# Layer 2 of a graph stack: pairs of tiles times two weights at once, in seven block products

## The reference

```python
def _L2_gnn_ref(X, A, Wv, bv, aw, ab, Wk, bk):
    Xw = X @ Wv + bv
    sj = Xw @ aw[:d, 0]
    si = Xw @ aw[d:, 0]
    e = leaky_relu(sj[:, None, :] + si[:, :, None] + ab[0], negative_slope=0.2)
    alpha_matrix = A * exp(e)
    transition = alpha_matrix / (sum(alpha_matrix, axis=-1, keepdims=True) + 1e-12)
    H = 0; Xk = X
    for k in range(3):
        H = H + Xk @ Wk[k] + bk[k]
        Xk = einsum('bij,bjd->bid', transition, Xk)
    return relu(H)
```

## Time and profile before

| | us |
|---|---|
| median of 3 runs | 2690.77 (2690.70 to 2690.77) |
| the profiled execution | 2691.02 |
| its span, first to last instruction | 2689.2 |
| TensorE busy | 2649.0 (99%) |
| VectorE busy | 1896.2 (71%) |
| ScalarE busy | 1217.6 (45%) |
| GpSimd busy | 1153.2 (43%) |

### The profile page before, as it was taken

How to read it: one execution, slowest core, us unless ns; L and a number is a source line. 1 busy time by engine, 2 the same in 40 slices (tenths; PEclk the granted TensorE clock), 3 DMA queues, 4 the chain that set the end, 5 groups by cost and what they waited for, 6 DMA issues and landing times.

```text
span 2689.2 us, 44559 instructions
## 1 busy us (share of the span) xinstructions
PE 2649.0 (99%) x13154; PEld 2210.4 (82%) x13154; DVE 1896.2 (71%) x4376; ACT 1217.6 (45%) x2231; POOL 1153.2 (43%) x2022
## 2 busy tenths in 40 slices
PE   7999999999999999999999999999999999999999
PEld 4888888888888888888888887888888888888887
DVE  7777777777777665666666657777777777777776
ACT  4444444444444554545445454323223222666665
POOL 5444443444444634343333346212212122677776
PEclk9999999999999999999999999999999999999999
DMA  4111111111111312111211123111111112344443
GB/s 135 41 37 47 41 37 37 42 46 37 38 36 45 98 46 67 33 66 36 64 41 59 45 73 102 58 55 54 51 57 49 55 55 64 114 148 152 137 138 123
DMA packets 136299, 178.58 MB, mean 66 GB/s; under 512 B 54464, under 2 KB 54464, under 8 KB 136256
## 3 DMA queue, kind: packets, MB, share of 16 engines
q1 hardware_dynamic: 131072, 168.62, 19.5%
q10 hardware_dynamic: 5184, 9.44, 1.2%
HBM read 110.90 MB, written 67.11 MB: 66 GB/s over the span
## 4 chain that ended last, share of the span: by engine, by line
PE 94%; DVE 2%; ACT 1%; issue 1%; POOL 1%; DMA 0%; SPq 0%; POOLq 0%; ACTq 0%; DVEq 0%
PE ps L461 27%; PE ps L463 27%; PE ps L462 27%; PE ps L478 6%; PE ps L503 4%; PE ps L481 2%; POOL w_lo L1261 1%; ACT row_hi L695 0%; DVE row_lo L945 0%; ACT w_hi L695 0%; PE ps L581 0%; PE ps L577 0%; DMA raw<-w0a 0%; POOL vecs L1286 0%; DVE adj_both L945 0%
## 5 line engine op out<-in xcount | busy, mean ns | idle before, releaser
L461 PE MATMUL ps<-w_hi,col_hi 128*128 128x512 f32 x2752 | 1100.8, 400 | 3.5 <-POOL w_lo L1261 1.0
L463 PE MATMUL ps<-w_hi,col_lo 128*128 128x512 f32 x2752 | 1075.4, 391 | 0.0
L462 PE MATMUL ps<-w_lo,col_hi 128*128 128x512 f32 x2752 | 1072.5, 390 | 0.0
L463 PEld LDWEIGHTS ps<-w_hi,col_lo 128*128 128x128 f32 x2752 | 516.8, 188 | 112.9
L461 PEld LDWEIGHTS ps<-w_hi,col_hi 128*128 128x128 f32 x2752 | 517.1, 188 | 109.9 <-issue 5.1
L462 PEld LDWEIGHTS ps<-w_lo,col_hi 128*128 128x128 f32 x2752 | 518.3, 188 | 98.5 <-issue 0.2
L1294 POOL TENSOR_TENSOR var_eps<-moments,eps_ln 128x1 f32<-128x1 f32 x256 | 55.6, 217 | 918.8 <-DVE moments L962 918.8
L695 ACT ACTIVATE col_hi<-ps 128x512 fp32r<-128x512 f32 x448 | 255.8, 578 | 257.2 <-PE ps L481 134.0
L949 DVE TENSOR_TENSOR wide<-ps,col_hi 128x512 f32<-128x512 f32 x256 | 175.5, 686 | 146.8 <-ACT col_hi L695 145.3
L695 ACT ACTIVATE row_hi<-ps 128x512 fp32r<-128x512 f32 x224 | 133.3, 595 | 305.7 <-PE ps L463 304.3
L1261 POOL TENSOR_TENSOR row_lo<-normed,row_hi 128x512 fp32r<-128x512 f32 x128 | 165.2, 1301 | 214.1 <-ACT row_hi L695 214.1
(11 more groups left out here) (151 smaller groups left out, 4095.1 us busy)
## 6 DMA issues: line engine op xcount, KB each, us to landing
out<-x_res SPq DMA_DIRECT2D x256, 256.0 KB, 2.0
x_in<-out SPq DMA_DIRECT2D x192, 256.0 KB, 2.8
x_in<-x SPq DMA_DIRECT2D x64, 256.0 KB, 2.6
x_res<-out SPq DMA_DIRECT2D x64, 256.0 KB, 3.1
adj_in<-adj_t SPq DMA_DIRECT2D x96, 64.0 KB, 2.4
raw<-w ACTq DMA_DIRECT2D x12, 256.0 KB, 2.7
raw<-wk ACTq DMA_DIRECT2D x12, 256.0 KB, 2.7
raw<-w_t ACTq DMA_DIRECT2D x10, 256.0 KB, 3.0
```

Of the source, the lines that this page charges most:

```text
L461: nc.tensor.matmul(out_ap, lhs_hi, rhs_hi, start=start, stop=False, **checks)
L462: nc.tensor.matmul(out_ap, lhs_hi, rhs_lo, start=False, stop=False, **checks)
L463: return nc.tensor.matmul(out_ap, lhs_lo, rhs_hi, start=False, stop=stop, **checks)
```

## The change

In layer 2, Wk2 and Wk1 are put side by side and a pair of tiles is multiplied by both in the seven block products of layer 3 (`halved` on each engine now serves both layers; `seventh` takes the layer). `lin2` and `lin1` go; `lin0` stays a linear per tile.

- The lists of layers 1 to 3 are new, and the last groups' lists of all four are written out. In layer 2's the products of one pair of tiles stand between the mixes and `lin0` of the other.
- `sj`, `alpha` and `tt` work on pairs: two transposes in a row, one step of ACT over both tiles.
- The score with vi: POOL multiplies (step `score`), ACT sums; DVE keeps the one with vj.
- `seed`: ACT copies the bias `bk` into the bank of `lin0` before it starts. `adj0`: ACT takes the relu, POOL adds the residual, which is now loaded by SP (`load_residual`) instead of copied.
- `adj1`: DVE adds the mix to the corner, ACT and POOL split the sum.
- The normalisation writes in place (`x_in`), and the loads of the next group's x wait for the transposes and scores.
- Weights: 32 operands in `STEPS`, made at places of the lists given in `STAGING` (layer, group, place): twelve in layer 1's groups 0 and 1, six in its last group, two in layer 2's first, and the twelve of `FINAL` (layer 3's) in layer 2's last group, each into the place of a layer 2 operand once the last pair's product has used it (`TAKES`). DVE makes the differences (`make`), ACT the high part, POOL the low part (`stage`).
- Group 1 also runs outside the loop, which now covers groups 2 to 14.

```diff
 def order_diffuse():
     return [
...
+        ("stats_n", 0), ("seed", 1), ("p1", 1), ("p2", 1), ("stats_n", 1), ("adj1", 0), ("adj1", 1), ("p6", 1),
+        ("seed", 0), ("norm_n", 0), ("p5", 1), ("lin0", 1), ("norm_n", 1), ("seed", 3), ("c11", 1), ("s5", 1),
+        ("sj", 1), ("alpha", 1), ("lin0", 0), ("score_n", 0), ("score_n", 1), ("tr_n", 0), ("p7", 1), ("c11h", 1),
+        ("c22", 1), ("sums_n", 0), ("tt", 1), ("tr_n", 1), ("adj0", 0), ("adj0", 1), ("p3", 1), ("sumsplit_n", 0),
+        ("p4", 1), ("stats_n", 2), ("c21", 1), ("p1_n", 0), ("stats_n", 3), ("seed", 2), ("p2_n", 0), ("c11_n", 0),
+        ("norm_n", 2), ("adj1", 2), ("p6_n", 0), ("adj1", 3), ("s5_n", 0), ("norm_n", 3), ("sj_n", 0), ("alpha_n", 0),
+        ("lin0", 3), ("score_n", 2), ("score_n", 3), ("c22_n", 0), ("p5_n", 0), ("lin0", 2), ("tr_n", 2),
+        ("sums_n", 1), ("adj0", 2), ("tr_n", 3), ("p7_n", 0), ("tt_n", 0), ("adj0", 3), ("p3_n", 0), ("c11h_n", 0),
+        ("sumsplit_n", 1), ("c21_n", 0), ("p4_n", 0),
     ]
...
 # module
+QUARTERS = ("B11", "B12", "B21", "B22")
+EARLY = [(2, op, j) for j in range(2) for op in ("B21", "B11", "T1", "T2", "T3", "T4")]
+LATE = [(2, "W0", j) for j in range(4)] + [(2, "B22", j) for j in range(2)] + [(3, "B11", j) for j in range(2)]
+FINAL = [(3, op, j) for j in range(2) for op in ("B21", "T1", "T2", "T3", "B22", "T4")]
+STEPS = EARLY + LATE + FINAL
+OPERAND_AT = {step: (1 + q // 4, q % 4) for q, step in enumerate(EARLY)}
+OPERAND_AT |= {(2, "W0", j): (4, j) for j in range(4)}
+OPERAND_AT |= {(layer, op, j): (0, 2 * (layer - 2) + j) for layer, op, j in LATE if op != "W0"}
+TAKES = {"B21": ("B11", "p1"), "T1": ("B21", "p2"), "T2": ("T2", "p6"), "T3": ("T1", "p5"), "B22": ("T3", "p7"),
+         "T4": ("T4", "p4")}
+OPERAND_AT |= {(3, op, j): OPERAND_AT[2, TAKES[op][0], j] for layer, op, j in FINAL}
+LOADS = ([(2, op, j) for j in range(2) for op in QUARTERS] + LATE + [(3, op, j) for j in range(2) for op in QUARTERS])
+BATCHES = [(0, 4, 0), (4, 8, 6), (8, 12, 12), (12, 14, 14), (14, 16, 16), (16, 20, 20), (20, 24, 26)]
+STAGING = {
+    (1, 0): {22: "load0", 39: 0, 48: 1, 49: 2, 57: 3, 60: 4},
+    (1, 1): {8: 5, 12: "load1", 25: 6, 28: 7, 29: 8, 44: 9, 56: 10, 60: 11},
+    (1, -1): {5: "load2", 16: 12, 21: 13, 31: 14, 34: 15, 51: "load3", 66: 16, 68: 17},
+    (2, 0): {0: "load4", 25: 18, 35: 19},
+    (2, -1): {4: "load5", 9: 20, 11: 21, 16: 22, 17: 23, 20: 24, 22: 25, 31: "load6", 35: 26, 37: 27, 38: 28, 39: 29,
+              43: 30, 45: 31},
+}
...
 # all engines
         def groups(eng, layer, body):
-            body(layer, 0, ORDERS[layer])
-            with eng.Fori(1, GROUPS - 1) as g:
+            for g in range(2):
+                body(layer, g, ORDERS[layer])
+            with eng.Fori(2, GROUPS - 1) as g:
                 body(layer, g, ORDERS[layer])
             body(layer, GROUPS - 1, LAST[layer])
...
 # SyncE
             def load_x(layer, g, t):
-                if layer == 3 and not first(g):
-                    sp.wait_ge(s["norm"], nl(layer, g, t) - SLOTS)
+                if layer == 3 or layer == 2 and not first(g):
+                    sp.wait_ge(sp2["tr"], nt(layer, g, t) - SLOTS)
+                    if layer == 2 or first(g):
+                        sp.wait_ge(s2["s_j"], nt(layer, g, t) - SLOTS)
+                        sp.wait_ge(s2["s_p"], nt(layer, g, t) - SLOTS)
                 elif layer > 0 or not first(g):
...
-                if layer == 3:
+                if layer >= 2:
                     for t in range(SLOTS):
-                        load_residual(g, t)
+                        load_residual(layer, g, t)
...
 # TensorE
+            def halved(layer, g, name, t):
+                u = t
+                a, b = 2 * u, 2 * u + 1
+                if name == "tr":
+                    pe.wait_ge(s["norm"], nl(layer, g, t))
+                    if layer == 2 and first(g):
+                        pe.wait_ge(s1["adj2_lo"], n(FULL, t))
+                    elif layer == 2 or first(g):
+                        pe.wait_ge(s2["row1"], nt(layer, g, t) - SLOTS)
+                    elif t % 2 == 0:
+                        pe.wait_ge(s3["c12"], np_(2, g, t // 2) - 2)
+                    else:
+                        pe.wait_ge(s3["mixed"], n(g, t) - SLOTS)
+                    transposes(t, x_in[:, t, :]).then_inc(sp2["tr"], 1)
+                if name == "p1":
+                    pe.wait_ge(sp2["tr_lo"], nt(layer, g, a))
+                    if layer == 2 and first(g):
+                        pe.wait_ge(s["final"], nl(2, g, a) - SLOTS)
+                    elif layer == 2 or first(g):
+                        pe.wait_ge(s2["relu"], nt(layer, g, a) - SLOTS)
+                    else:
+                        pe.wait_ge(sp2["rowb_lo"], np_(layer, g, u) - 2)
+                    if first(g):
+                        wait_operand(pe, layer, "B11")
+                    seventh(layer, (a, 1), col_hi[:, a, 0:2 * P], col_lo[:, a, 0:2 * P], "B11").then_inc(sp2["products"], 1)
...
             def diffuse(g, name, t, i):
+                u = t // 2
+                halved(2, g, name, t)
+                if name == "sj":
+                    u = t
+                    pe.wait_ge(s2["s_j"], n(g, 2 * u + 1))
+                    wait_pair(pe, "sums", "s1", 2, g, u)
+                    pe.wait_ge(sp2["tr_lo"], nt(2, g, 2 * u + 1))
+                    for h in range(2):
+                        last = nc.tensor.transpose(scores_at(u)[:, h, :],
+                                                   score[:, S_J, 2 * u + h:2 * u + h + 1].to_broadcast([P, P]), ident[:])
+                    last.then_inc(s2["sj"], 1)
+                if name == "tt":
+                    u = t
+                    pe.wait_ge(s2["alpha"], 6 * np_(2, g, u))
+                    for h in range(2):
+                        last = nc.tensor.transpose(transitions_at(u)[:, h, :], edge(2 * u + h), ident[:])
+                    last.then_inc(s2["tt"], 1)
+                if name == "adj1":
+                    pe.wait_ge(s2["tt_lo"], np_(2, g, u))
+                    pe.wait_ge(sp2["rowb_lo" if t % 2 else "rowa_lo"], np_(2, g, u))
+                    mix(0, t, start=t % 2 == 1).then_inc(s2["adj1"], 1)
+                if name == "lin0":
+                    wait_pair(pe, "seeded", "b" if t % 2 else "a", 2, g, u)
                     if first(g):
+                        wait_operand(pe, 2, "W0")
+                    linear(1, t, OPERAND_AT[2, "W0", 0][0], start=False, stop=False, skip_group_check=True)
                 if name == "adj0":
                     pe.wait_ge(s2["row1_lo"], i)
                     mix(1, t, start=False).then_inc(s2["adj0"], 1)
...
 # ScalarE
+            def load_weights(batch):
+                start, end, done = BATCHES[batch]
+                if batch == 0:
+                    wait_split(act, block_end[1])
+                else:
+                    act.wait_ge(sw["lo"], done)
+                for i in range(start, end):
+                    b = block_end[1] + i
+                    act.dma_start(raw_of(i), source(i)).then_inc(raw_loaded[b % RAW], 16)
+            def stage(step):
+                layer, op, j = STEPS[step]
+                place, k = OPERAND_AT[layer, op, j]
+                if STEPS[step] in FINAL:
+                    wait_pair(act, "products", TAKES[op][1], 2, FULL, 1)
+                elif op == "W0":
+                    act.wait_ge(s1["lin0"], TILES)
+                elif (op, layer) == ("B22", 2):
+                    act.wait_ge(s1["lin2"], TILES)
                 if op[0] == "T":
+                    act.wait_ge(sw["made"], made_by(step))
                 else:
+                    wait_load(act, load_of(step))
+                copy(w_hi[:, place, k, :], full_of(step)).then_inc(sw["hi"], 1)
...
+                if name == "seed":
                     if first(g):
+                        act.wait_ge(s["bk_sum"], 2)
+                    if t % 2:
+                        wait_pair(act, "corners", "c11", 2, g, u)
                     else:
+                        act.wait_ge(sp2["rowb_lo"], np_(2, g, u))
+                    copy(ps[:, t, 1, :], bk_bc[:]).then_inc(s2["seeded"], 1)
+                if name == "adj1":
+                    act.wait_ge(s2["row1"], i)
+                    copy(row_hi[:, t, :], c22_at(u) if t % 2 else c12_at(u)).then_inc(s2["row1_hi"], 1)
+                if name == "adj0":
+                    act.wait_ge(s2["adj0"], i)
+                    relu(wide[:, t, 0:F], ps[:, t, 1, :]).then_inc(s2["relu"], 1)
...
 # VectorE
+                if name == "score":
+                    dve.wait_ge(s["norm"], nl(2, g, t))
+                    if not first(g):
+                        dve.wait_ge(s2["sj"], np_(2, g, t // 2) - 2)
+                    if t > 0 or not first(g):
+                        dve.wait_ge(s2["s_j"], i - 1)
+                    V.scalar_tensor_tensor(scratch, x_in[:, t, :], 0.0, vj_bc[:], ALU.max, ALU.mult,
```

(48 more changed lines are left out.)

680 lines of the change are left out of this document (302 added, 378 removed), and 34 rows, old and new, of the table LEAK.

## The result

The changed kernel takes **2645.55 us** (median of 4 runs, 2644.62 to 2646.03) where the kernel before takes 2690.77 (2690.70 to 2692.01) beside it: ratio 0.983, 95% interval 0.9813 to 0.9847. The forecast was 2645.0. That it lies 0.55 us off is partly luck: two of its terms are wrong by 8 us and 4 us with opposite signs, and a gain of 3.6 us wasn't in it at all. The span went from 2689.2 to 2644.2 us, 45.0 less, and the rest of this text accounts for those 45.0.

The account below looks back on a forecast made before the run. The prediction took PE's matmuls to bound the kernel. Its terms -43.5 - 1 - 4 + 3 = -45.5 took 2691.0 to 2645.5 us in the profile, 2645 us as median; range 2635 to 2664 us.

Parts of the forecast that it names:

- Matmuls removed: Layer 2's groups: 192 fewer matmuls on PE at 0.2266 us each, -43.5 us.
- Joined transposes: Score and transition transposes issued two tiles at a time: 0 to 7 us saved, taken as -1.
- Entry into layer 2: First two groups of layer 2: of 8.2 us lost, 0 to 12 would be left, taken as 4, so -4.
- The chain over B22: Entry into layer 2: ACT and POOL copies of B22 take 3.8 us, against 5.3 us of PE work before p3.
- Entry into layer 3: Layer 2's last group: POOL makes twelve operands, 34.4 us against PE's 30.5; cost 0 to 8 us, taken as +3.
- the residual's path: Layer 2's groups: residual lands at 17.8 us, POOL's queued steps end at 21.7, p6 starts at 22.5; fits by 0.8 us.
- Layer 3 steady: Layer 3's steady groups: no term in the sum; PE was read as 99.7% busy there.
- Other engines' work and steady chains: Layer 2's steady groups: POOL 27.8, ACT 26.0, DVE 26.4 us under PE's 38.3, and chains fit; cost 0.
- An engine decides only from 38.3 us on: Layer 2's steady groups: other engines cost nothing below PE's 38.3 us a group, leaving POOL 10.5 us more.
- 1: Rival: a steady chain of layer 2 comes late, sj to tt or p6, 0.8 us a group; 2658 us, chance 0.18.
- 3: Rival: residual load lands late and holds POOL, 2.9 us a group loses the gain; at 4 us 2709, chance 0.04.
- Rival 2: Entries into layers 2 and 3 cost more, 12 and 8 us with 1.2 GHz matmuls behind; 2658 us, chance 0.12.

Follow-up runs that it names:

- experiment 1: Changed kernel with layer 2's product p5 issued twice, 192 matmuls more in all: 2683.64 us.
- experiment 9: Changed kernel with ACT's copy of T4's first half moved two places down the list of layer 2's last group: 2645.84 us.
- experiment 8: Changed kernel with the last four weight loads of layer 3 issued by SP ahead of its stores instead of by ACT: 2643.67 us.
- 6: Changed kernel with POOL writing only 8 of 512 columns of the low parts of layer 3's twelve last operands: 2641.82 us.
- 7: Changed kernel with DVE subtracting only 8 of 512 columns in the eight differences T1 to T4 of layer 3's weights: 2646.18 us.
- 10: Changed kernel with residual loads ahead of load_adj, last weight loads on SP ahead of the stores, and T4's first half moved behind c21: 2641.97 us.
- experiment 2: Kernel before with only layer 3's list order_mean taken from the changed kernel: 2688.07 us.
- experiment 11: Changed kernel with POOL's score product x_in * vi issued twice in layer 2, 5.2 us more a group: 2684.72 us.
- 4: Changed kernel with layer 2's four residual loads issued in the order 3, 2, 1, 0: 2689.61 us.

## Why the prediction was right, and where it was not

1. **Matmuls removed, -43.5:** right. Count 192, steady PE 100% busy; a group lost 2.77 us against 2.72 of matmuls, and experiment 1 gives 2.65 to 2.72 back. Measured -44.3 with the next point. The 0.2158 us set beside it is not a figure for such a stretch: the Trainium skill ("TensorE: Matmul & The Clock Gate", Back-to-back issue gap) gives that formula for a matmul on its own. The trace's 0.2266 us is what held.
2. **Joined transposes, -1:** right. What is left of the 2.77 is 0.05 a group, 0.8 in all.
3. **Entry into layer 2, -4:** -8.2. The bound was "0 to 12 left"; a wait of 0.7 us is left. The chain over B22, which was costed at 3.8 against 5.3, did fit. That the twelve operands made early brought the rest is likely, but no run shows it by itself.
4. **Entry into layer 3, +3: this step failed.** It cost +10.6, beyond its upper bound of 8. The sum compared POOL's 34.4 us with PE's 30.5, and took the difference as the wait. What it had no term for:
   - ACT's place in between: its copy waits for DVE's subtraction, and the transition matrix queues behind the copy, 3.0 us. With one copy moved (experiment 9) 1.8 are left.
   - ACT's four DMA issues, 2.66 us, of the wait of 3.3. Without them (experiment 8) that wait is gone.
   - The subtractions at 1.48 and 1.60 us instead of 0.68, with POOL beside them.
   - Seven matmuls at the 1.2 GHz level, 7 x 0.2 = 1.4.

   POOL's lateness itself, which the term was about, is at most the third wait, 1.6 us. The profile names no releaser for it ("issue"), but PE starts at 2263.10 and the first half of POOL's low part of the sums, begun at 2261.73, ends by its usual 1.28 us at 2263.0; this is inferred from the times. In the residual's path the prediction counted what is queued behind a wait on POOL; on ACT it didn't count it here. Which share each has stays open in part: experiments 6, 7, 8 and 9 each relieve one place, and the next wait or the slow matmuls take back some or all of it. With three edits of order together (10) 7.9 of the 10.6 are left.
5. **Layer 3 steady, 0:** -3.6, from a wait of a quarter of a microsecond a group that no list named; experiment 2 shows it by itself.
6. **Other engines' work and steady chains, 0:** right for the kernel as it is, and for POOL and DVE nearly to the digit (27.4 and 26.2 us a group by the window, forecast as 27.8 and 26.4; ACT 23.9 for 26.0). Wrong in the margin. "An engine decides only from 38.3 us on, 10.5 us more of POOL": 5.2 us more, placed beside the score chain, cost 39 us. "It fits by 0.8 us": it fits by 0.2.
7. **The rivals.** None came to pass in full. But the mechanisms of 1 and 3 are there: 5.2 us more of POOL bring the first (experiment 11), 2.8 us more of POOL's wait for the load the third (4), each at the price of nearly the whole gain. Rival 2 was half right: one entry cost more, the other less.

With the measured sizes the forecast would read -44.3 - 8.2 + 10.6 - 3.6 + 0.5 = -45.0, against -45.5 as written. The nearness is luck in this: the entry into layer 3 was 7.6 us too cheap, the other entry 4.2 too dear, and 3.6 came from a list that was not looked at.
